# Fp32 sums as multiply-adds and a new split of the bilinear sampling, in a deformable convolution block on one core

## What is computed

```python
off = conv([w_offx; w_offy], x)           # 18 values a pixel: dy and dx for each of 9 taps
py = dy + (h - 1 + ky); px = dx + (w - 1 + kx)
y0, x0 = floor(py), floor(px); ty, tx = py - y0, px - x0
s = x[y0, x0] * (1-ty)*(1-tx) + x[y0, x0+1] * (1-ty)*tx \
  + x[y0+1, x0] * ty*(1-tx)   + x[y0+1, x0+1] * ty*tx      # per tap; 0 outside the image
out_x, out_y = sum over taps of w_dx[tap] @ s, of w_dy[tap] @ s
out = relu(bn1(conv(concat(conv(x, w_normal), out_x, out_y), w_fusion)))
result = relu(bn2(conv(out, w_conv2)) + x)
```

## Time and profile before

| | us |
|---|---|
| median of 3 executions | 2666.21 |
| lowest, highest | 2661.54, 2680.01 |
| profiled execution | 2666.55 |
| its span, first to last instruction | 2664.7 |

### The profile page before, as it was taken

How to read it: one execution, slowest core, us unless ns; L and a number is a source line. 1 busy time by engine, 2 the same in 40 slices (tenths; PEclk the granted TensorE clock), 3 DMA queues, 4 the chain that set the end, 5 groups by cost and what they waited for, 6 DMA issues and landing times.

```text
span 2664.7 us, 46973 instructions
## 1 busy us (share of the span) xinstructions
PE 2356.6 (88%) x15680; PEld 2317.9 (87%) x15680; DVE 2250.6 (84%) x5999; ACT 1564.2 (59%) x3577; POOL 2005.8 (75%) x1807
## 2 busy tenths in 40 slices
PE   3667989989998999999999998998899999989997
PEld 3667988988998989899899988998899989989997
DVE  5788888888998988988889888998898988988862
ACT  5777877787655555555555555555555555555541
POOL 7778777777777777777777777777777777777740
PEclk7789999999999999999999999999999999999999
DMA  7766777777777777777777777766666666667640
GB/s 225 212 209 204 233 228 224 228 224 223 222 223 238 228 227 234 223 232 236 235 223 240 234 237 227 237 204 196 206 203 209 192 206 207 199 198 207 192 130 25
DMA packets 179138, 564.89 MB, mean 212 GB/s; under 512 B 32720, under 2 KB 34128, under 8 KB 178768
## 3 DMA queue, kind: packets, MB, share of 16 engines
q0 software_dynamic: 144000, 471.97, 59.4%
q1 hardware_dynamic: 34896, 89.91, 9.6%
HBM read 527.41 MB, written 34.34 MB: 211 GB/s over the span
## 4 chain that ended last, share of the span: by engine, by line
DVE 37%; PE 28%; ACT 12%; DMA 11%; issue 9%; POOL 4%; ACTq 0%; DVEq 0%; POOLq 0%; SPq 0%
DVE mixed L756 9%; DMA cells<-slope_table,index 8%; PE work L388 6%; PE work L394 6%; PE work L391 6%; DVE d_lo L708 5%; DVE samp L762 5%; ACT samp L535 4%; DVE samp_lo L708 4%; POOL cells L350 4%; ACT samp_hi L534 3%; PE turned L431 3%; DMA cells<-in_xpair,index 2%; PE acc L388 2%; PE acc L391 2%
## 5 line engine op out<-in xcount | busy, mean ns | idle before, releaser
L350 POOL DMA_INDIRECT cells<-slope_table,index x1350 | 1488.8, 1103 | 411.7 <-issue 203.9
L535 ACT ACTIVATE samp<-mixed,wgt 128x128 f32<-128x128 f32 x1800 | 648.2, 397 | 601.4 <-DVE mixed L756 598.4
L756 DVE SCALAR_TENSOR_TENSOR mixed<-cells,wgt 128x256 f32<-128x256 f32 x1350 | 574.8, 476 | 158.4 <-DMA cells<-slope_table,index 155.6
L350 POOL DMA_INDIRECT cells<-in_xpair,index x450 | 507.3, 1127 | 149.5 <-issue 86.1
L388 PE MATMUL work<-d_hi,w_hi 128*128 128x320 f32 x1440 | 478.9, 333 | 77.7 <-ACT off_s L534 73.6
L762 DVE SCALAR_TENSOR_TENSOR samp<-mixed,wgt,samp 128x128 f32<-128x128 f32 x1800 | 515.5, 345 | 31.4 <-ACT samp L535 30.8
L391 PE MATMUL work<-d_lo,w_hi 128*128 128x320 f32 x1440 | 462.3, 321 | 0.0
L394 PE MATMUL work<-d_hi,w_lo 128*128 128x320 f32 x1440 | 462.3, 321 | 0.0
L388 PE MATMUL acc<-samp_hi,w_hi 128*128 128x320 f32 x1440 | 450.1, 313 | 0.0
L391 PE MATMUL acc<-samp_lo,w_hi 128*128 128x320 f32 x1440 | 447.9, 311 | 0.0
L394 PE MATMUL acc<-samp_hi,w_lo 128*128 128x320 f32 x1440 | 446.5, 310 | 0.0
(11 more groups left out here) (90 smaller groups left out, 4232.9 us busy)
## 6 DMA issues: line engine op xcount, KB each, us to landing
cells<-slope_table,index POOLq DMA_INDIRECT x1350, 3.9
slope<-in_xpair SPq DMA_DIRECT2D x54, 384.0 KB, 5.4
slope_table<-slope SPq DMA_DIRECT2D x54, 384.0 KB, 4.0
x_raw<-in_xflat SPq DMA_DIRECT2D x40, 410.0 KB, 4.5
resid<-in_x SPq DMA_DIRECT2D x40, 320.0 KB, 5.3
out<-resid SPq DMA_DIRECT2D x40, 320.0 KB, 4.0
cells<-in_xpair,index POOLq DMA_INDIRECT x450, 3.9
w_lo_f<-in_weights SPq DMA_DIRECT2D x4, 576.0 KB, 8.0
```

Of the source, the lines that this page charges most:

```text
L350: eng.indirect_dma_start(out=cells[:, g, :], out_offset=None, in_=cell_rows, in_offset=bass.IndirectOffsetOnAxis(ap=index[:, par, j, k:k + ...
L535: return eng.activation(dst, src, ACT.Copy, scale=scale)
L756: eng.scalar_tensor_tensor(out=both, in0=corner[:, g, :, 1, :], scalar=wgt[:, par, 1, 0, j, k:k + 1], in1=base, op0=ALU.mult, op1=ALU.add, ...
```

## The change

- Every fp32 tensor_tensor of sums, zs, last_row and slopes becomes combine: scalar_tensor_tensor with a factor of 1.0, (a * 1.0) + b or - b. The subtractions that write low parts (L708) stay as they are.
- In images 1 to 3 (n >= PLAIN) ACT makes both horizontal products in place in mixed, 10 instructions a tap (across), and DVE adds the halves with one combine of 640 values (blend) in place of five scalar_tensor_tensor. samp_done then counts one a tap, left_done ten. In image 0 the arithmetic of the sampling is as before.
- sample is split in mix and blend. In tap n DVE now does blend(n + 2), samples_low(n + 1), indices at k = fl.turn, and then mix(n + 3), ahead of the finished jobs. ACT does samples_high(n + 1), turned_evac at k = fl.turn, across(n + 3), upper(n + 4), and then the finished jobs.
- The start of the kernel is written out to match.

```diff
+TOTAL = NS * TAPS
+
+PLAIN = STRIPS * TAPS
...
+def left_count(n):
+
+    return TILES * min(n, PLAIN) + 2 * TILES * max(n - PLAIN, 0)
...
+def samp_count(n):
+
+    return TILES * min(n, PLAIN) + max(n - PLAIN, 0)
...
-                at_least(eng, samp_done, TILES * n + TILES)
+                at_least(eng, samp_done, samp_count(n + 1))
...
+            def upper(n):
+                if n >= PLAIN:
                     return
 
-                at_least(eng, samp_done, TILES * (n - 1))
+                c, k, tp = n // TAPS, n % TAPS, n % 2
+                at_least(eng, samp_done, samp_count(n - 1))
...
                     copy(mixed[:, tp, j].rearrange("p (x c) -> p x c", x=2), corner[:, g, :, 0, :],
...
+            def across(n):
+                if n >= TOTAL:
+                    return
+
+                c, k, tp = n // TAPS, n % TAPS, n % 2
+                if n < PLAIN:
+                    at_least(eng, samp_turned, n - 1)
                 for j in range(TILES):
                     at_least(eng, mixed_done, TILES * n + j + 1)
-                    copy(samp[:, tp, j], mixed[:, tp, j, 0:C], scale=wgt[:, par, 0, 1, j, k:k + 1]).then_inc(left_done, 1)
+                    left, right = mixed[:, tp, j, 0:C], mixed[:, tp, j, C:2 * C]
+                    if n < PLAIN:
+                        copy(samp[:, tp, j], left, scale=wgt[:, c % 2, 0, 1, j, k:k + 1]).then_inc(left_done, 1)
+                    else:
+                        copy(left, left, scale=wgt[:, c % 2, 0, 1, j, k:k + 1]).then_inc(left_done, 1)
+                        copy(right, right, scale=wgt[:, c % 2, 1, 1, j, k:k + 1]).then_inc(left_done, 1)
...
-                    if fl.strip and k < TAPS - 2:
-                        left(n + 2, k + 2, par, tp)
-                    elif fl.strip and fl.nxt:
-                        left(n + 2, k + 2 - TAPS, 1 - par, tp)
...
-                    if fl.strip and k < TAPS - 3:
-                        upper(n + 3, i, k + 3, par, 1 - tp)
-                    elif fl.strip and fl.nxt:
-                        upper(n + 3, i + 1, k + 3 - TAPS, 1 - par, 1 - tp)
                     if k == fl.turn and fl.nxt:
                         turned_evac(i + 1)
+                    across(n + 3)
+                    upper(n + 4)
...
-            def sample(n, k, par, tp):
-
+            def combine(dst, a, b, op):
+
+                return eng.scalar_tensor_tensor(out=dst, in0=a, scalar=1.0, in1=b, op0=ALU.mult, op1=op)
+
+            def mix(n):
+                if n >= TOTAL:
+                    return
+
...
+                    if n < PLAIN:
                         at_least(eng, upper_done, TILES * n + j + 1)
                     else:
-                        at_least(eng, cells_in[g], (PER // GSLOTS * 16) * (n // TAPS) + 16 * turns)
...
                     eng.scalar_tensor_tensor(
-                        out=both, in0=corner[:, g, :, 1, :], scalar=wgt[:, par, 1, 0, j, k:k + 1], in1=base,
+                        out=both, in0=corner[:, g, :, 1, :], scalar=wgt[:, c % 2, 1, 0, j, k:k + 1], in1=base,
...
+            def blend(n):
+                if n >= TOTAL:
+                    return
+
+                c, k, tp = n // TAPS, n % TAPS, n % 2
+                if n >= PLAIN:
+                    at_least(eng, samp_turned, n - 1)
+                    at_least(eng, left_done, left_count(n + 1))
+                    combine(samp[:, tp], mixed[:, tp, :, 0:C], mixed[:, tp, :, C:2 * C], ALU.add).then_inc(samp_done, 1)
+                    return
...
-                    eng.tensor_tensor(to[:, SUM_ROW:SUM_ROW + PAIRS, :], even, odd, ALU.add).then_inc(sums_done, 1)
-                    eng.tensor_tensor(to[:, DIFF_ROW:D_ROWS, :], odd, even, ALU.subtract).then_inc(sums_done, 1)
+                    combine(to[:, SUM_ROW:SUM_ROW + PAIRS, :], even, odd, ALU.add).then_inc(sums_done, 1)
+                    combine(to[:, DIFF_ROW:D_ROWS, :], odd, even, ALU.subtract).then_inc(sums_done, 1)
...
-                    eng.tensor_tensor(to[:, 1:HR, :], raw[:, g, 0:HR - 1, :], raw[:, g, 2:HR + 1, :],
-                                      ALU.subtract).then_inc(zs_done, 1)
-                    eng.tensor_tensor(to[:, HR:Z_ROWS - 1, :], raw[:, g, HR - 1:ROWS - 2, :], raw[:, g, HR + 1:ROWS, :],
-                                      ALU.subtract).then_inc(zs_done, 1)
+                    combine(to[:, 1:HR, :], raw[:, g, 0:HR - 1, :], raw[:, g, 2:HR + 1, :], ALU.subtract).then_inc(zs_done, 1)
+                    combine(to[:, HR:Z_ROWS - 1, :], raw[:, g, HR - 1:ROWS - 2, :], raw[:, g, HR + 1:ROWS, :],
+                            ALU.subtract).then_inc(zs_done, 1)
...
-                    ins = eng.tensor_tensor(to[:, :, 0, :], keep[:, :, 1, :], raw[:, :, 1, :], ALU.subtract)
+                    ins = combine(to[:, :, 0, :], keep[:, :, 1, :], raw[:, :, 1, :], ALU.subtract)
...
-                    ins = eng.tensor_tensor(to, keep[:, :, 0, :], raw[:, :, 0, :], ALU.subtract)
+                    ins = combine(to, keep[:, :, 0, :], raw[:, :, 0, :], ALU.subtract)
...
-                eng.tensor_tensor(slope[:, :, 1], slope[:, :, 1], slope[:, :, 0], ALU.subtract).then_inc(slope_done, 1)
+                combine(slope[:, :, 1], slope[:, :, 1], slope[:, :, 0], ALU.subtract).then_inc(slope_done, 1)
...
-                    if fl.strip and k < TAPS - 2:
-                        sample(n + 2, k + 2, par, tp)
-                    elif fl.strip and fl.nxt:
-                        sample(n + 2, k + 2 - TAPS, 1 - par, tp)
+                    blend(n + 2)
                     if fl.strip and (k < TAPS - 1 or fl.nxt):
...
                     if k == fl.turn and fl.nxt:
                         indices(i + 1, 1 - par)
+                    mix(n + 3)
```

More of the change, by code:

```diff
@@ L567, in upper @@
                     copy(mixed[:, tp, j].rearrange("p (x c) -> p x c", x=2), corner[:, g, :, 0, :],
-                         scale=wgt[:, par, 0, 0, j, k:k + 1]).then_inc(upper_done, 1)
-            def left(n, k, par, tp):
-                at_least(eng, samp_turned, n - 1)
+                         scale=wgt[:, c % 2, 0, 0, j, k:k + 1]).then_inc(upper_done, 1)
+            def across(n):
[4 more added lines that the diff above has]
+                    at_least(eng, samp_turned, n - 1)
                 for j in range(TILES):
                     at_least(eng, mixed_done, TILES * n + j + 1)
-                    copy(samp[:, tp, j], mixed[:, tp, j, 0:C], scale=wgt[:, par, 0, 1, j, k:k + 1]).then_inc(left_done, 1)
+                    left, right = mixed[:, tp, j, 0:C], mixed[:, tp, j, C:2 * C]
[4 more added lines that the diff above has]
+                        copy(right, right, scale=wgt[:, c % 2, 1, 1, j, k:k + 1]).then_inc(left_done, 1)
             def samples_high(n, tp):
@@ L597, in _ @@
             weights_high(W_DEF)
-            upper(0, 0, 0, 0, 0)
-            left(0, 0, 0, 0)
+            upper(0)
+            across(0)
             x_high(1, 1)
-            upper(1, 0, 1, 0, 1)
+            upper(1)
+            across(1)
+            upper(2)
             samples_high(0, 0)
-            left(1, 1, 0, 1)
-            upper(2, 0, 2, 0, 0)
+            across(2)
+            upper(3)
             eng.wait_ge(bn_step, 1)
@@ L763, in sample @@
                         out=samp[:, tp, j], in0=mixed[:, tp, j, C:2 * C],
-                        scalar=wgt[:, par, 1, 1, j, k:k + 1], in1=samp[:, tp, j], op0=ALU.mult, op1=ALU.add,
+                        scalar=wgt[:, c % 2, 1, 1, j, k:k + 1], in1=samp[:, tp, j], op0=ALU.mult, op1=ALU.add,
                     ).then_inc(samp_done, 1)
@@ L801, in _ @@
             weights_low(W_DEF)
-            sample(0, 0, 0, 0)
+            mix(0)
+            blend(0)
             x_low(1, 1)
-            sample(1, 1, 0, 1)
+            mix(1)
+            blend(1)
             samples_low(0, 0)
+            mix(2)
             eng.wait_ge(bn_in, 16)
```

5 lines of the change are left out of this document (2 added, 3 removed).

## The result

| | before | after |
|---|---|---|
| median, us | 2665.14 (2661.54 to 2680.01, 4 runs) | 2808.32 (2804.68 to 2813.87, 4 runs) |
| span of the profiled execution, us | 2664.7 | 2812.1 |
| ratio after / before | | 1.0522, 95% interval 1.0496 to 1.0548 |

The forecast was 2568 us with a range of 2525 to 2705. The time lies outside it, and on the other side of before.

A forecast was written before the change was run, and what follows sets the result against it. POOL, issuing gathers without a pause, was taken as the bound. Its terms, 97 + 30 + 30 - 28 = 129 us less, gave 2536 us; PE and DVE's heavy taps allowed up to 2600; the middle, 2568 us, was forecast, range 2525 to 2705.

The forecast's parts named there:

- The bound of before: POOL issues gathers without a pause; its long ones are held by back-to-back fp32 TENSOR_TENSOR runs on DVE.
- 97 + 30 + 30 = 157 us: POOL's saving: 97 us from long gathers in images 1 to 3, about 30 from followers, 30 in image 0.
- On POOL it can be all or nothing ... I take the best: Sums in multiply-add form: gathers wait for one instruction's rest, some 0.2 us, not a run; worst case 0 us or more.
- the hold stays and grows: Rival: the new form holds POOL's port as before and blend lengthens runs; +40 us in images 1 to 3, 2705 us; chance 0.24.
- L708 runs never hold: d_lo subtractions on DVE: a gather starting in a run of six took 0.95 us, so they let gathers in.
- The term for blend: One sum a tap: gathers starting during blend are held 0.35 us on average, 48 us; net +28 us on POOL.
- PE needs samp_lo(n + 1) first, so that is the better order: Mixing three taps ahead: mix(n + 3) behind samples_low(n + 1) serves PE sooner; no cost counted.
- Taps 4 to 7: DVE's heavy taps of a strip: 27.1 us against PE's 25.8, keeping a strip at 60 to 61.5 us.
- ACT has room: Both products on ScalarE: ACT rises from 34.5 to 47.5 us a strip; room over a strip, not in each tap.
- The second rival: POOL's relief is real, but ACT and DVE take its place through waits for across; no change, 2660 us; chance 0.16.
- ACT's products 0.29 us apart: Both products on ScalarE: five more ACTIVATEs a tap at 0.29 us each, 392 us, 13 us a strip.
- DVE's busy time down by 167 for 175: One sum a tap in images 1 to 3: DVE saves 0.65 us a tap, 175 us of busy time.

The follow-up runs named there:

- e4_break: Before, with a one-value memset behind each of the 13 instructions of sums and zs on DVE; 2579.9 us, ratio 0.9661.
- e8_break_all: Before, with the one-value memset in all the runs: sums, zs, mix, the five multiply-adds, d_lo, low part of mid; 2566.0 us, ratio 0.9615.
- e1_form: Before, with the multiply-add form in sums, zs, last_row and slopes and nothing else; 2671.4 us, ratio 0.9993.
- e2_ahead: Before, with mixing three taps ahead and the new order in all images, but tensor_tensor sums, five products and five multiply-adds; 2832.1 us, ratio 1.061.
- e12_after_break_all: After, with all the memsets of e7_mix_first_break but mix(n + 3) left behind samples_low(n + 1) and indices; 2801.0 us, ratio 1.0491.
- e7_mix_first_break: After, mix(n + 3) ahead of samples_low(n + 1), memsets behind instructions of mix, image 0's blend, sums, zs, d_lo, mid's low part; 2540.5 us.
- e3_split: Before, with ten products on ACT and one sum a tap on DVE in images 1 to 3, in the old order; 2832.8 us, ratio 1.0607.
- e5_after_break: After, with a one-value memset behind each DVE instruction of sums, zs and both d_lo runs; 2782.4 us, ratio 1.0425.
- e11_one_input: Before, with 12 of the 13 instructions of sums and zs made one-input copies; 2582.5 us in one execution.

## Why the prediction was wrong, point by point

**The bound of before: right.** That POOL issues without a pause and that back-to-back runs on DVE hold its long gathers was read from the earlier trace rows. e4_break and e8_break_all bear it out: memsets that compute nothing give back 90 and 103 us (by the ratios). The prediction put 97 + 30 + 30 = 157 us on the holds beside sums and zs and their followers; e4_break got 90 us from just these places. So even where the relief is real, a little over half of it comes back. Some of the rest is held by other runs (34 gathers in the mixing), and PE, at 94% in e4_break, is not far behind.

**The form: wrong, and it carried the forecast.** Step "On POOL it can be all or nothing ... I take the best" is the first that failed: -157 us should have been 0, as e1_form shows (0.9993). The evidence was there. The two L947 in the new form stood inside a held stretch, which is a direct observation of the form at work; against it I set a statistic, that gathers begun in a scalar_tensor_tensor are rarely held over more than one. That statistic compared different runs at different phases and not the two forms. The rule of the Trainium skill that spoke against it (SBUF — State Buffer, Who interferes with whom: two SBUF inputs contend, whatever the operation) has the trace on its side, with 46 of 52 long gathers in the new form. I named it and gave it 0.24; it deserved most of the chance.

**The rival "the hold stays and grows": its mechanism right, its price too small.** The hold does run on through blend, 3.93 us where it was 3.14. It was priced at 40 us; durations above the median grew by 284 - 206 = 78 us, and images 1 to 3 by 81 us. What was missing are the 32 gathers held in d_lo runs with 72 us. The prediction took it as settled from one gather in the earlier trace rows that L708 runs never hold. They do in e2_ahead (53 times) with the order alone. The term for blend was good: 138 gathers by 0.35 us were expected, some 140 with 45 us came.

**The order: costed at nothing, and it costs the most.** The sentence "PE needs samp_lo(n + 1) first, so that is the better order" is the second step that failed. It looks at PE alone. ACT, which in the same tap goes samples_high, then across, needs the first mix of n + 3 as its next input; with mix behind samples_low, and samples_low behind samples_high, ACT must wait for DVE's answer to what it has just sent. The two queues were written out, and walking one tap through both would have shown it: 0.74 us for samp_lo and 0.48 for the first mix, 1.2 us of ACT's wait (measured 1.28), and where indices stand between the two 3.3 us more (measured 4.29 in all, since ACT fills 0.4 us of it with its copy of off_s). e12_after_break_all against e7_mix_first_break shows it for one line alone, 260 us. e2_ahead and image 0 of after, where there is no split and POOL pauses, agree: 5.4 us a strip in image 0, 58 us. In images 1 to 3 of after POOL's longer holds stand at the same height, so the 81 us there belong to both bounds: taking away one gains at most 1.0 us a strip.

**Taps 4 to 7 and "ACT has room": beside the point.** The sum held engines against each other by how long they are busy. DVE and ACT ended at 74% and 68% and still set a bound (in image 0 the only one), through waits of one on the other. The second rival had this (DVE waiting for across, 1.4 us) but in one direction only, which is what e3_split shows (2.0 us, 489 us in all). In after it is 91.7 us. The other direction, which no rival named, is DVE's wait for samp_hi, 210.1 us.

**What was right in size.** ACT's products 0.29 us apart (ten in 3.04 us), blend behind another instruction 0.81 to 0.82 us long and started 0.73 apart from the next (0.75 taken), PE's off_s waits gone (though 50 us for off_c came in their place), DVE's busy time down by 167 for 175. None of it set the time.

**How the parts add up.** By the ratios: form 0 (e1_form); order +6.1% (e2_ahead); split, once the order is there, -0.9%. That is 5.2%, the measured difference. These are steps along one way through the variants; by the other, the split first costs 6.1% (e3_split) and the order then gives 0.9% back. And with gathers let in and mix(n + 3) first, order and memsets alone bring 5.1%, the split nothing.

## What to carry to other kernels

Where two engines hand a tile to and fro, write one period of both queues side by side and follow the data round: an input that stands behind a job which itself waits for the other engine closes a loop, and its price is in no busy share. When removing one cause does little or nothing, look for a second bound at the same height before dropping it; here the two were worth 26 and -4 us alone and 268 together (with some more memsets). Where GpSimd issues indirect transfers all the time, look at its longest instructions beside VectorE's back-to-back runs, and try a memset of one value in the run before rewriting the arithmetic.

## What was not expected of the hardware

- A gather can be held not for one instruction but through a whole run without a gap on DVE: 3.30 and 3.93 us where an undisturbed one takes 0.95. That of 1333.85 ends at 1337.15, 0.90 us behind the start of samp_lo at 1336.25, which takes one of its inputs (turned) from PSUM. The Trainium skill (SBUF — State Buffer, Who interferes with whom) has the first to issue keep the port pair for its instruction; the trace shows the hold last over several instructions.
- With a memset of 128 x 1, 59 ns long, behind each instruction of the run the hold is gone (e5_after_break: none of 1.9 us or more in images 1 to 3). In sums it puts the next instruction some 0.01 us later (0.41 us apart in place of 0.40). The same section has an instruction with at most one SBUF input, outside the two-port modes, leave the pair alone, and this agrees.
- The same operation holds a gather or doesn't with its pace: a tensor_scalar of 325 ns for 320 values holds, one of 386 ns for 240 does not (e11_one_input). The section names the two-port modes as contending too; if the double pace is such a mode, which no row says, this agrees.
- Open: why a gather begun at one moment of a run is held to its end while another, in the same kind of run, is held only for what is left of one instruction. And with it, why d_lo runs hold none in images 1 to 3 of before and 32 in after. The starting moment within the instruction may decide it: the 18 of e11_one_input all begin 0.01 to 0.03 us behind the start of the first L837 of a run. But of before's gathers with such a start in other instructions many are not held, and no run here varied the moment alone.
